# A one-core decoder layer with two sorts of the tokens: a running maximum chooses the expert, and the second sort gets a new order of roots, ranks, norms and pad rows

## The reference: what is computed

```python
x = layernorm(x + attention(x))                 # low-rank scores, one softmax for all heads
x = layernorm(x + expert_by_token_id(x, ids))   # 4 experts, chosen by ids // 3125, weights = ctx
x = layernorm(x + ffn_top1(x))                  # 4 experts, chosen by the router

logits = x @ Wr + br                            # (1024, 4)
probs = softmax(logits); top_w, top_idx = top_k(probs, 1)
h = silu(x @ Wg[e]) * (x @ Wu[e]); y = h @ Wd[e]   # e = top_idx of the token, F = 1024
out = y[top_idx] * top_w
```

## Time and profile before

| | |
|---|---|
| runs, us | 196.77, 197.69, 198.11 |
| span of the profiled execution, us | 194.3 (the page gives no other time of it) |
| TensorE busy | 176.0 us, 91% |
| VectorE, ScalarE, GpSimd busy | 68%, 53%, 53% |
| second stage starts on TensorE | 42.49 us |
| first product of the FFN, in the chain of waits | 76.39 us |

### The profile page before, as it was taken

How to read it: one execution, slowest core, us unless ns; L and a number is a source line. 1 busy time by engine, 2 the same in 40 slices (tenths; PEclk the granted TensorE clock), 3 DMA queues, 4 the chain that set the end, 5 groups by cost and what they waited for, 6 DMA issues and landing times.

```text
span 194.3 us, 3905 instructions
## 1 busy us (share of the span) xinstructions
PE 176.0 (91%) x969; PEld 140.0 (72%) x969; DVE 132.0 (68%) x406; ACT 103.3 (53%) x274; POOL 103.0 (53%) x130
## 2 busy tenths in 40 slices
PE   1999997999999898989999999999999999999810
PEld 0677775447888655668888788888888888888610
DVE  3269996895678887536554454444799986888950
ACT  3136776725567935537664946643665422455530
POOL 7006356770126884627772168860588810377683
PEclk9999999999999999999999999999999999999975
DMA  5999999246999223146544105444050000011010
GB/s 157 359 336 418 378 366 319 73 139 168 322 334 405 101 85 94 29 130 173 221 149 150 46 0 165 164 162 167 0 162 3 0 0 3 0 57 56 22 62 24
DMA packets 15317, 29.14 MB, mean 150 GB/s; under 512 B 1726, under 2 KB 11968, under 8 KB 15170
## 3 DMA queue, kind: packets, MB, share of 16 engines
q1 hardware_dynamic: 13568, 25.68, 39.4%
q0 software_dynamic: 1440, 3.22, 4.7%
q10 hardware_dynamic: 290, 0.01, 0.1%
HBM read 20.41 MB, written 9.28 MB: 153 GB/s over the span
## 4 chain that ended last, share of the span: by engine, by line
PE 68%; POOL 11%; issue 7%; DMA 5%; DVE 3%; ACT 3%; POOLq 1%; SPq 1%; DVEq 0%; ACTq 0%
PE bank L484 14%; PE bank L486 13%; PE bank L485 13%; POOL out_tokens L473 5%; PE bank L729 4%; PE bank L563 4%; PE bank L652 3%; PE bank L629 3%; POOL rstd L395 3%; DMA arena<-in_attn_w 3%; PE bank L594 2%; PE bank L572 2%; PE bank L511 2%; DMA x_sorted<-buf,slot 1%; PE bank L498 1%
## 5 line engine op out<-in xcount | busy, mean ns | idle before, releaser
L391 POOL TENSOR_TENSOR w_lo<-stage,w_hi 128x512 fp32r<-128x512 f32 x40 | 51.4, 1305 | 44.0 <-ACT w_hi L803 44.0
L912 ACT ACTIVATE gate<-bank 128x256 f32<-128x256 f32 x44 | 17.0, 387 | 48.5 <-PE bank L486 48.5
L1206 DVE TENSOR_TENSOR hid<-bank,gate 128x256 f32<-128x256 f32 x44 | 18.7, 425 | 30.5 <-ACT gate L912 30.2
L484 PE MATMUL bank<-w_hi,xr 128*128 x88 | 35.9, 408 | 1.4 <-DVE xr L1164 0.8
L486 PE MATMUL bank<-w_hi,xr 128*128 x88 | 34.7, 395 | 0.0
L485 PE MATMUL bank<-w_lo,xr 128*128 x88 | 34.7, 394 | 0.0
L484 PE MATMUL bank<-w_hi,hT 128*128 x88 | 28.5, 324 | 0.7 <-DVE hT L1211 0.7
L803 ACT ACTIVATE w_hi<-stage 128x512 fp32r<-128x512 f32 x48 | 28.6, 630 | 0.3 <-PE bank L486 0.3
L486 PE MATMUL bank<-w_hi,hT 128*128 x88 | 24.9, 282 | 0.0
L485 PE MATMUL bank<-w_lo,hT 128*128 x88 | 24.8, 282 | 0.0
L484 PEld LDWEIGHTS bank<-w_hi,xr 128*128 128x128 f32 x88 | 16.6, 189 | 4.4 <-issue 2.3
(11 more groups left out here) (182 smaller groups left out, 329.7 us busy)
## 6 DMA issues: line engine op xcount, KB each, us to landing
stage<-in_w_ffn SPq DMA_DIRECT2D x16, 768.0 KB, 4.5
rows<-x_sorted SPq DMA_DIRECT2D x22, 132.0 KB, 2.3
x_sorted<-padrow SPq DMA_DIRECT2D x1, 2244.0 KB, 10.2
x_sorted<-padrow SPq DMA_DIRECT2D x1, 2112.0 KB, 16.4
buf<-in_x_tok SPq DMA_DIRECT2D x1, 1024.0 KB, 11.0
w_hi<-in_ctx SPq DMA_DIRECT2D x1, 1024.0 KB, 11.5
w_hi<-in_ctxT SPq DMA_DIRECT2D x1, 1024.0 KB, 14.0
x_sorted<-padrow SPq DMA_DIRECT2D x1, 792.0 KB, 12.7
```

What stands on the lines that cost most here:

```text
L391: g.tensor_tensor(out=lo, in0=src, in1=hi.bitcast(F32), op=ALU.subtract).then_inc(split_lo, 1)
L484: mm(dst, xhi, whi, start=start, stop=False)
L912: a(gate[:, (T + j) % 2, :], fA[j % 2][:, 0:FQ], ACT.Silu).then_inc(silu_done, 1)
L1206: v.tensor_tensor(out=hid[:, (T + j) % 2, :], in0=fA[j % 2][:, FQ:2 * FQ], in1=gate[:, (T + j) % 2, :], op=ALU.mult).then_inc(h_done, 1)
```

## The change

- **Choice.** A logit row is stored between a lowest value and the token's number (`choice`, six wide: low, four logits, token). One `tensor_tensor_scan` over the group makes a running maximum: with `min` against `cap` (lowest at each tile's first element, highest elsewhere) the maximum begins anew at each tile. Two more steps follow: where is the running maximum equal to its last value, and the difference of neighbours, which marks the first such place. For this the token number is stored as (1024 + number) times -2^100, below any logit, and that of a pad row as 2^126, above all, which marks the fifth column.
- **Root.** `ve2` (variance + eps) is made by VectorE behind `bn_aggr`, so `root2` is one GpSimd instruction. The root is written into the row (column `RSTD`) and travels with it. `nmr2` (minus mean times root) is one VectorE instruction of `choose`; ScalarE's `shift2` goes.
- **Softmax weight.** The shifted logits, formerly by-products of `choose`, are made in the FFN by four VectorE steps (`shifted_logits`), and `gates` decodes the token number in two steps.
- **Pad rows.** SP issues the second pad DMA right behind the first, ahead of the eleven row loads.
- **Order.** `choose(n)` comes ahead of a residual and `place(n)` ahead of a `hidden` on VectorE; `rank(n)` right behind an `up` on TensorE; `norm2` of single tiles ahead of `silu` or behind `h1copy` on ScalarE; on GpSimd the roots are moved among the scatters. Offset tables of tiles 0 to 2 move behind residual(10).

```diff
...
     sp.dma_start(pads2[:, 0:HALF2, :], padrow[:].unsqueeze(1).broadcast_to([P, HALF2, ROW])).then_inc(d_init2, 16)
+    sp.dma_start(pads2[:, HALF2:BLOCKS2, :],
+                 padrow[:].unsqueeze(1).broadcast_to([P, BLOCKS2 - HALF2, ROW])).then_inc(d_init2, 16)
...
         sp.dma_start(rows[:, t, :], scr1[t * P:(t + 1) * P, :]).then_inc(d_rows[t], 16)
...
         sorted_rows(t)
-    sp.dma_start(pads2[:, HALF2:BLOCKS2, :],
-                 padrow[:].unsqueeze(1).broadcast_to([P, BLOCKS2 - HALF2, ROW])).then_inc(d_init2, 16)
...
-    def validity():
-
+    def move_tokens():
...
-        g.tensor_copy(buf[:, :, TOK], rows[:, :, TOK]).then_inc(valid_step, 1)
-        g.tensor_scalar(out=valid[:], in0=rows[:, :, TOK], scalar1=float(TOKENS), scalar2=None,
-                        op0=ALU.is_lt).then_inc(valid_step, 1)
-        pool.wait_ge(valid_step, 2)
-        g.tensor_tensor(out=prio2[:], in0=prio[:].unsqueeze(1).broadcast_to([P, T, E]),
-                        in1=valid[:].unsqueeze(2).broadcast_to([P, T, E]), op=ALU.mult).then_inc(valid_ready, 1)
+        g.tensor_copy(choice[:, :, E + 1], rows[:, :, TOK]).then_inc(tok_moved, 1)
+        g.tensor_copy(buf[:, :, TOK], rows[:, :, TOK]).then_inc(tok_moved, 1)
...
-        pool.wait_ge(aggr2_ready, n + 1)
-        g.tensor_scalar(out=ve2[:, a:b], in0=mv2[:, a:b, 1], scalar1=EPS, scalar2=None,
-                        op0=ALU.add).then_inc(pool_step, 1)
-        pool.wait_ge(pool_step, n + 1)
+        pool.wait_ge(ve2_ready, n + 1)
...
-    validity()
+    move_tokens()
+    pool.wait_ge(tok_moved, 2)
     root2(0)
+    pool.wait_ge(d_init2, 32)
+    scatter2(0)
     root2(1)
-    pool.wait_ge(d_init2, 32)
-    for t in range(0, 3):
+    for t in range(1, 4):
         scatter2(t)
     root2(2)
-    for t in range(3, ROUTED):
+    for t in range(4, ROUTED):
         scatter2(t)
     root2(3)
+    scatter2(7)
     root2(4)
-    for t in range(ROUTED, T):
+    for t in range(8, T):
         scatter2(t)
     for q in range(NQ):
...
+        if i in RANK_AT:
+            rank(RANK_AT[i])
...
-        if i == 7:
-            rank(0)
-        if i == 9:
-            rank(1)
...
-        if i == 10:
-            rank(2)
+    idle_products(4)
+    rank(3)
...
-    rank(3)
-    idle_products(6)
...
-        act.wait_ge(shift2_ready, t + 1)
+        act.wait_ge(nmr2_ready, GROUP_OF[t] + 1)
...
-
-    def shift2(n):
-        s, e = GROUPS[n]
-        act.wait_ge(rstd2_ready, n + 1)
-        a(nrs2[:, s:e], rstd2[:, s:e], ACT.Copy, scale=-1.0).then_inc(nrs_ready, 1)
-        act.wait_ge(nrs_ready, n + 1)
-        for t in range(s, e):
-            a(nmr2[:, t:t + 1], mv2[:, t, 0:1], ACT.Identity, scale=nrs2[:, t:t + 1]).then_inc(shift2_ready, 1)
...
-    SHIFT_AT = {6: 0, 9: 1, 10: 2}
-    NORMS_AT = {7: (0, 1), 8: (2,), 9: (3, 4), 10: (5, 6)}
+    NORM_BEFORE_SILU = {6: 0, 7: 2, 8: 3, 10: 5}
+    NORM_BEHIND_COPY = {6: 1, 8: 4, 10: 6}
...
+        if i in NORM_BEFORE_SILU:
+            norm2(NORM_BEFORE_SILU[i])
...
-        if i in SHIFT_AT:
-            shift2(SHIFT_AT[i])
-        for t in NORMS_AT.get(i, ()):
-            norm2(t)
-    for t in ADDED_BY_PE:
-        evict(t)
-    for n in range(GROUP_OF[ROUTED], len(GROUPS)):
-        shift2(n)
-        for t in range(*GROUPS[n]):
-            norm2(t)
+        if i in NORM_BEHIND_COPY:
+            norm2(NORM_BEHIND_COPY[i])
+    evict(9)
+    norm2(7)
+    evict(10)
+    norm2(8)
...
-        last = v.bn_aggr(mv2[:, t, :], stats[:, t % 2, :])
+        step(v.bn_aggr(mv2[:, t, :], stats[:, t % 2, :]))
...
-            last.then_inc(aggr2_ready, 1)
+            s, e = GROUPS[GROUP_ENDING[t]]
+            v.scalar_tensor_tensor(out=ve2[:, s:e], in0=mv2[:, s:e, 1], scalar=EPS, in1=ones_f[:, 0:e - s],
+                                   op0=ALU.add, op1=ALU.mult).then_inc(ve2_ready, 1)
     def choose(n):
...
-        lm = buf[:, a:b, LOG:LOG + E]
...
-            dve.wait_ge(valid_ready, 1)
+            dve.wait_ge(tok_moved, 1)
+            dve.wait_ge(tok_ready, 2)
...
-        step(v.tensor_tensor(out=logit[:, a:b, :], in0=lm,
-                             in1=rstd2[:, a:b].unsqueeze(2).broadcast_to([P, w, E]), op=ALU.mult))
-        step(v.tensor_tensor(out=logit[:, a:b, :], in0=logit[:, a:b, :],
-                             in1=br_all[:].unsqueeze(1).broadcast_to([P, w, E]), op=ALU.add))
-        step(v.tensor_reduce(out=lmax[:, a:b], in_=logit[:, a:b, :], axis=AX.X, op=ALU.max))
-        step(v.tensor_tensor(out=lm, in0=logit[:, a:b, :],
-                             in1=lmax[:, a:b].unsqueeze(2).broadcast_to([P, w, E]), op=ALU.subtract))
-        step(v.scalar_tensor_tensor(out=lw[:, a:b, 0:E], in0=lm, scalar=0.0, in1=prio2[:, a:b, :],
-                                    op0=ALU.is_ge, op1=ALU.mult))
-        step(v.tensor_reduce(out=lwmax[:, a:b], in_=lw[:, a:b, :], axis=AX.X, op=ALU.max))
-        v.tensor_tensor(out=m2[:, a:b, :], in0=lw[:, a:b, :],
-                        in1=lwmax[:, a:b].unsqueeze(2).broadcast_to([P, w, E + 1]),
-                        op=ALU.is_equal).then_inc(mask_ready, 1)
+        v.scalar_tensor_tensor(out=nmr2[:, a:b], in0=mv2[:, a:b, 0], scalar=-1.0, in1=rstd2[:, a:b],
+                               op0=ALU.mult, op1=ALU.mult).then_inc(nmr2_ready, 1)
+        for t in range(a, b):
+            v.scalar_tensor_tensor(out=choice[:, t, 1:E + 1], in0=buf[:, t, LOG:LOG + E], scalar=rstd2[:, t:t + 1],
+                                   in1=br_all[:], op0=ALU.mult, op1=ALU.add).then_inc(logit_ready, 1)
+        dve.wait_ge(logit_ready, b)
+        step(v.tensor_tensor_scan(out=run[:, a:b, :].rearrange("p t e -> p (t e)"),
+                                  data0=cap[:, 0:w, :].rearrange("p t e -> p (t e)"),
+                                  data1=choice[:, a:b, :].rearrange("p t e -> p (t e)"),
+                                  initial=LOW, op0=ALU.min, op1=ALU.max))
+        step(v.tensor_tensor(out=at_max[:, a:b, :], in0=run[:, a:b, :],
+                             in1=run[:, a:b, E + 1:E + 2].broadcast_to([P, w, E + 2]), op=ALU.is_equal))
+        v.tensor_tensor(out=m2[:, a:b, :], in0=at_max[:, a:b, 1:E + 2], in1=at_max[:, a:b, 0:E + 1],
+                        op=ALU.subtract).then_inc(mask_ready, 1)
     def place(n):
...
+    CHOOSE_AT = {GROUPS[n][1] + 2: n for n in range(3)}
+    PLACE_AT = {GROUPS[n][1] + 3: n for n in range(3)}
     for i in range(T):
+        if i in PLACE_AT:
+            place(PLACE_AT[i])
         hidden(i)
-        if i == 7:
-            residual(5)
-            choose(1)
-        elif i == 9:
-            residual(7)
-            choose(2)
-        else:
-            if i == 10:
-                place(2)
-            if i >= 2:
-                residual(i - 2)
-            if i == 5:
-                choose(0)
-            if i == 6:
-                place(0)
-            if i == 8:
-                place(1)
+        if i in CHOOSE_AT:
+            choose(CHOOSE_AT[i])
+        if i >= 2:
+            residual(i - 2)
...
+    choose(3)
...
+    place(3)
...
-    choose(3)
-    place(3)
+    offset_tables(0, EARLY)
...
+    def shifted_logits():
+        step(v.tensor_tensor(out=logit[:], in0=rows[:, :, LOG:LOG + E],
+                             in1=rows[:, :, RSTD:RSTD + 1].broadcast_to([P, T, E]), op=ALU.mult))
+        step(v.tensor_tensor(out=logit[:], in0=logit[:], in1=br_all[:].unsqueeze(1).broadcast_to([P, T, E]),
+                             op=ALU.add))
+        step(v.tensor_reduce(out=lmax[:], in_=logit[:], axis=AX.X, op=ALU.max))
+        v.tensor_tensor(out=lshift[:], in0=logit[:],
+                        in1=lmax[:].unsqueeze(2).broadcast_to([P, T, E]), op=ALU.subtract).then_inc(lshift_ready, 1)
+
...
-        step(v.tensor_copy(outidx[:], rows[:, :, TOK]))
+        step(v.scalar_tensor_tensor(out=tok_abs[:], in0=rows[:, :, TOK], scalar=-1.0, in1=rows[:, :, TOK],
+                                    op0=ALU.mult, op1=ALU.max))
+        step(v.tensor_scalar(out=outidx[:], in0=tok_abs[:], scalar1=-1.0 / TOK_SCALE, scalar2=float(-TOK0),
+                             op0=ALU.mult, op1=ALU.add))
...
```

56 lines of the change are left out of this document (37 added, 19 removed).

## The result

| | before | after |
|---|---|---|
| median, us | 197.23 (196.10 to 198.11) | 205.26 (203.77 to 205.84) |
| ratio | 1 | 1.040, 95% interval 1.036 to 1.044 |
| span of the profiled execution, us | 194.3 | 202.0 |

The forecast was 200.9 with a range up to 203.2: the sign was right, the size was not, and the time lies outside the range. The two profiled executions lie 7.7 apart and stand for the medians' 8.0. The page of the changed kernel says where to look: TensorE has two products fewer to do (967 against 969) and is busy 1.2 us longer (177.2 against 176.0), so the 7.7 are times at which it was slow or had nothing.

What follows compares the result with a forecast made beforehand. TensorE, busy 91%, bounds the kernel, so tx(0)'s start and the way to fup(0) decide. Early pads +2.1 and the handover's order +1.1 make 3.2 on 197.69: 200.9 us, own range 199.8 to 202.3, wider range 198.2 to 203.2.

Steps and rivals of the forecast that it cites:

- Three to four scatters share the engines meanwhile: 1.3: First sort: scatters of 0.4 us each add 1.3 us to the second pad transfer, which then ends at 44.25.
- Term 1: Early pads ahead of rows 0 in SP's queue delay tx(0): +2.1 us, bounds 0 and +4.6.
- rows 0's landing: First sort: rows 0 land some 0.4 behind the pads, at 44.65; as a sign of being right, 44 to 45.5.
- Clock, booked at 0: TensorE's granted clock: no loss booked for the 1.5 us wait at rank(4), since shorter waits had left it at 1.00.
- Term 2: Second sort's new order, tx(0) to fup(0): fup(0) at 77.45 instead of 76.39, +1.1 us, bounds +0.6 and +1.9.
- Root 3 is ready at 70.85, against 71.72 today: 0.9 won: Second sort, GpSimd: the new order has root 3 ready 0.9 us earlier, a gain then lost before fup(0).
- my upper bound: Second sort: waits before a scatter at 0.80 us, which would make the handover term +1.9.
- The FFN's extra VectorE work: shifted_logits and gates add 0.8 and 0.2 us on VectorE, hidden behind fup: 0, without cover at most 1.0.
- the DMA share: Sign of being right: the DMA share stays near 1 until about 42 us.
- the way from `tx(0)` to the FFN's first product: Sign of being right: from tx(0) to fup(0) takes 34.5 to 35.8 us.
- the gap in the FFN: Sign of being wrong: a gap of over 0.5 us within the FFN that was not there.
- the scatters are held too: Rival: pads also hold the first sort's scatters, scatter 5 landing at 44.3; +4.6 and +1.1, 203.4; chance 0.10.

Runs made afterwards that it cites:

- e4: Changed kernel, early pads kept, with rows 0 to 2 issued from ScalarE's queue instead of SP's; 205.41 us, ratio 1.039.
- e1: Changed kernel with the second pad transfer put back behind the eleven row loads; 200.18 us, ratio 1.016.
- e2: Kernel before with only the second pad transfer moved up behind the first; 201.76 us, ratio 1.022.
- e13: Changed kernel with ranks 0 to 2 behind th, places 0 to 2 behind hidden, and root 4 ahead of scatter 7; 204.70 us, ratio 1.039.
- e5: Changed kernel with 20 idle products instead of 5 ahead of tx(0); 202.93 us, ratio 1.029.
- e11: Changed kernel with the second pad transfer split, half early and half behind the row loads; 200.78 us, ratio 1.018.
- e10: New arithmetic in the old order, but root 3 ahead of scatter 6, choose(3) ahead of residual(10), offset steps later, fewer idle products; 197.72 us, ratio 1.004.
- e7: Changed kernel with pads back behind the row loads, root 1 ahead of the pad wait, root 4 ahead of scatter 7; 199.19 us, ratio 1.018.
- e16: e3 with GpSimd's roots ahead of the scatters and ranks and places a whole tile later, as in the kernel before; 197.02 us, ratio 1.006.
- e3: Changed kernel with pads back, root 1 ahead of the pad wait, and the token decode steps moved into shifted_logits; 199.25 us, ratio 1.016.
- e8: Changed kernel's new arithmetic with every order as in the kernel before, decode steps moved into shifted_logits; 195.15 us, ratio 0.996; again 195.99 us, 0.997.
- e9: Changed kernel with ranks 0 to 2 on TensorE behind th instead of ahead of it; 204.43 us, ratio 1.037.
- e12: Changed kernel with ranks 0 to 2 behind th on TensorE and places 0 to 2 behind hidden on VectorE; 205.58 us, ratio 1.045.
- e14: Changed kernel with half the second pads early, ranks and places later, root 4 ahead of scatter 7, decode steps moved; 199.90 us, ratio 1.015.

## Why the prediction was wrong

**The step that failed: "Three to four scatters share the engines meanwhile: 1.3", with scatter 5 itself on time.** Term 1 asked when SP's queue lets rows 0 through and took the scatters as extra load on the pads. The load ran the other way: SP issues rows 0 only when scatter 5 has landed, and scatter 5 took 5.84 instead of 2.45. e4 shows that the queue's order adds nothing to scatter 5's wait, e1 and e2 that the pads are worth 4.4 to 5.1 where I had 2.1. My estimate of rows 0's landing, 44.65, came out not far from the 45.34 in the chain of waits, by luck: the pads' end (44.25 forecast, 43.86 in e13) was right, but the rows were held by something else. The rows for the right one were in the prediction: landings of 2.4 to 6.7 with full engines. I had put that case at 0.10 and 203.4, as a bound for rows 0 and not as the mechanism; since the two longest, 6.7 and 5.8, are those of the scatters issued beside the first half of the pads, and the 2.4 that of one beside nearly idle engines, it should have been the first case.

**Clock, booked at 0, measured 1.0.** I had looked at waits of up to 0.6 in the trace, behind which the clock was 1.00, and didn't ask what a wait of 2 us ahead of `tx(0)`, which my own forecast contained, would do., which I named for it, is a window in which TensorE never waits. Behind 3.56 of idleness the clock fell to 0.50. e5 shows the size. How much idleness is enough the runs don't settle: the clock fell behind 1.89 in e11 and 1.86 in e10, and in e2's second sort behind 0.61 and 0.92, but not behind 1.92 at `rank(1)` in e1. Behind the wait of 1.67 before `rank(4)`, for which I had booked nothing, it stayed at 1.00, as forecast.

**Term 2, +1.1, measured +2.96.** The order of scatter 7 and root 4 was right and was worth what the step said: 1.1 (e7), in the chain of the profile as forecast. What failed is "Root 3 is ready at 70.85, against 71.72 today: 0.9 won". From `tx(0)`, root 3 ended 0.5 later than before, not 0.9 earlier, once the clock's 1.0 is taken out (76.19 - 45.48 - 0.95 = 29.76, before 71.72 - 42.49 = 29.23). The difference of 1.4 is, by my reading, TensorE's waits of 0.52, 0.55 and 0.55 at ranks 0 to 2, which I never wrote down: I followed GpSimd and VectorE, group by group, and took TensorE's own pace as given. e16 bears this out, though it moves GpSimd's roots too: without these waits root 3 ends 1.3 earlier from `tx(0)` than in e3 (29.3 against 30.5). From root 3's end on it was 7.10 instead of 6.60, through a `choose` of 1.06 and waits before a scatter of 0.8, my upper bound.

**The FFN's extra VectorE work, booked at 0, measured 0.8** (1.1 against the same kernel with the steps moved). I priced the two decode steps as free-running instructions of 0.2 and didn't look at what GpSimd does at that moment; held to 0.68 and 1.21, they outlast the cover of one `fup`. The uncovered bound of 1.0 was right by accident. `shifted_logits`, 0.8 at 112.1 to 113.0, did cost nothing, as forecast: the items around it keep their distance of about 2.3.

**Right:** choices of 1.06 instead of 1.38 (1.0 forecast), root without `ve`; the early pads' cost lies in the first handover; root 4 behind scatter 7, with the chain through it. Of the signs that were to show it right, the DMA share (1.04 from 40 to 42) and rows 0's landing (45.34) came, and the way from `tx(0)` to the FFN's first product did not: 37.8 by the chain, where 34.5 to 35.8 was forecast. Of the signs of being wrong one came, the gap in the FFN. Of the rivals, "the scatters are held too" named the cause. The arithmetic alone, in the order that it found (e8), is worth 0.3 to 0.4%; in both of its profiles the FFN is 0.46 shorter, which the decode's place would explain; the handover is 0.35 shorter in one and 0.52 longer in the other, so the profiles don't say where the rest lies.

**Open:** what of the up to 2 us by which the changed kernel's other executions exceed the profiled one isn't the clock's; how much idleness makes the clock fall; what holds a scatter's packets beside the pads, and which part of it comes last; whether the second decode step was held by its mode.

## What to carry to other kernels

Before a bulk transfer is moved into a stretch with small transfers on the critical path, read how long those take to land in a saturated stretch of the same trace: the small ones pay, though here the big one was in another queue. When instructions of one engine are moved ahead, follow every engine that waits for them at each place, the bottleneck's waits first; and where a chain goes A, B, A, C over two engines, fill A's wait for B with the work that the next chain needs. A wait of 3 us or more on TensorE cost the lower clock behind it on top of itself, 1 to 2 us here, which idle products in the wait bought back.

## What the runs showed of the hardware

- An indirect scatter of 135 kB that took 2.4 us to land took 5.8 to 6.1 with 1056-byte writes beside it, at a DMA share of 1.05 to 1.11 from 36 to 40 us, in seven executions, and 3.9 to 4.8 when those writes ended early; in the last case with the share down to 0.1 for its final 2 us.
- The granted clock went to 0.50 behind waits on TensorE of 3.0 to 4.8 us ahead of `tx(0)` in all six executions that had one (after, e2, e4, e9, e12, e13), stayed at 1.00 behind one of 1.36 (e14), and fell behind one of 1.89 (e11). In the second sort it stayed at 1.00 behind 1.92 (e1, `rank(1)`) and 1.67 (after, `rank(4)`), and fell behind 1.86 (e10) and behind 0.61 and 0.92 (e2). The length of the last wait alone doesn't tell.
- Two VectorE instructions of 0.17 took 0.68 and 1.21 beside GpSimd's `tensor_tensor` of 1.27, and ended with it; `tensor_reduce` and `reciprocal`, just ahead of them in the same stretch, took 0.19 and 0.23.
